# A cross-attention kernel on one core: the max rounds run four visits ahead of the exponent tiles instead of three

## The reference

```python
q, k, v = heads(x @ w_q), heads(text @ w_k), heads(text @ w_v)      # text: 1593 tokens
out_text = softmax(q @ k.T / sqrt(16)) @ v
out_ip   = softmax(q @ k_ip.T / sqrt(16) + mask) @ v_ip             # 8 tokens
out = (merge(out_text) + merge(out_ip)) @ w_out + b_out + x
```

## Time and profile before

| | |
|---|---|
| median of 3 runs (lowest to highest) | 1845.01 us (1843.49 to 1846.52) |
| profiled execution: its own time | 1848.91 us |
| profiled execution: span of the core's instructions | 1847.0 us |
| busy: PE, DVE, ACT, POOL | 1811.4, 1332.3, 1185.7, 382.6 us |
| mean granted TensorE clock | 0.993 |
| loop groups 0 to 38 begin | 79.88 to 1765.71 us after the span's start |

### The profile page before, as it was taken

One profiled execution on the slowest core, in us unless ns is written; L12 is line 12 of the kernel. 1 busy time (PEld: TensorE's weight loads), 2 busy tenths in 40 slices (PEclk: granted clock), 3 DMA queues, 4 the chain that ended last, 5 costly groups with the idle time before them and its releaser, 6 DMA issues.

```text
span 1847.0 us, 41069 instructions
## 1 busy us (share of the span) xinstructions
PE 1811.4 (98%) x16856; PEld 718.8 (39%) x16856; DVE 1332.3 (72%) x1787; ACT 1185.7 (64%) x2340; POOL 382.6 (21%) x508
## 2 busy tenths in 40 slices
PE   8999999999999999999999999999999999999988
PEld 3333333433344343433344333343333433434332
DVE  6777777778767787677876777777777777767871
ACT  1276666666666666666666666666666666666766
POOL 5112222211122121122121221112122122221000
PEclk9999999999999999999999999999999999999989
DMA  7555334363344434355453464435544364343410
GB/s 226 102 92 160 67 77 92 73 164 73 74 106 116 106 71 86 94 139 102 79 99 75 141 103 77 97 69 144 94 77 96 72 155 85 74 95 74 77 30 26
DMA packets 103806, 178.16 MB, mean 96 GB/s; under 512 B 42933, under 2 KB 71270, under 8 KB 103618
## 3 DMA queue, kind: packets, MB, share of 16 engines
q1 hardware_dynamic: 82658, 134.12, 37.3%
q0 software_dynamic: 18944, 40.10, 6.9%
q10 hardware_dynamic: 2016, 1.31, 0.2%
HBM read 117.63 MB, written 48.98 MB: 90 GB/s over the span
## 4 chain that ended last, share of the span: by engine, by line
PE 93%; DMA 2%; DVE 2%; SPq 1%; ACT 1%; issue 1%; POOL 0%; ACTq 0%; DVEq 0%; POOLq 0%
PE pv_bank L800 27%; PE max_bank L727 20%; PE work_bank L582 12%; PE exp_bank L784 12%; PE work_bank L604 11%; PE work_bank L627 3%; PE work_bank L593 2%; PE max_bank L745 2%; PE exp_bank L788 1%; DVE tile_max L1069 1%; DMA o_t<-o_sum 1%; SPq L475 1%; ACT probs L978 1%; PE work_bank L658 1%; PE work_bank L611 1%
## 5 line engine op out<-in xcount | busy, mean ns | idle before, releaser
L978 ACT ACTIVATE probs<-exp_bank 128x512 f32<-128x512 f32 x1908 | 1002.0, 599 | 417.3 <-PE exp_bank L784 410.2
L1069 DVE TENSOR_REDUCE tile_max<-max_bank 128x2 f32<-128x1024 f32 x632 | 773.4, 1224 | 400.5 <-PE max_bank L727 395.5
L727 PE MATMUL max_bank<-k_stack,q_stack 48*128 48x512 f32 x1896 | 567.9, 469 | 7.4 <-DVE tile_max L1069 7.3
L800 PE MATMUL pv_bank<-probs,v_ones 128*17 128x512 f32 x3840 | 518.1, 603 | 0.1
L1071 DVE TENSOR_REDUCE tile_max<-max_bank 128x1 f32<-128x512 f32 x632 | 430.2, 681 | 2.7 <-PE max_bank L727 2.7
L784 PE MATMUL exp_bank<-q_stack,k_stack 50*128 50x512 f32 x1908 | 415.9, 403 | 4.0 <-DMA q_stack<-neg_rows 2.7
L727 PEld LDWEIGHTS max_bank<-k_stack,q_stack 48*128 48x128 f32 x1896 | 234.0, 185 | 409.8 <-issue 269.6
L784 PEld LDWEIGHTS exp_bank<-q_stack,k_stack 50*128 50x128 f32 x1908 | 240.0, 188 | 63.2 <-ACT probs L978 47.2
L582 PE MATMUL work_bank<-ctxt,wk 128*32 128x400 f32 x2528 | 253.5, 506 | 7.6 <-DMA wk<-in_w_k 5.5
L604 PE MATMUL work_bank<-wv,ctxt 128*32 128x320 f32 x3040 | 254.0, 435 | 0.0
L604 PEld LDWEIGHTS work_bank<-wv,ctxt 128*32 128x32 f32 x3040 | 93.8, 109 | 163.1 <-issue 100.3
(11 more groups left out here) (124 smaller groups left out, 832.3 us busy)
## 6 DMA issues: line engine op xcount, KB each, us to landing
k_stack<-scratch_k SPq DMA_DIRECT2D x234, 199.2 KB, 6.9
scratch_k<-k_parts SPq DMA_DIRECT2D x80, 400.0 KB, 4.6
ctxt<-in_ctx_t POOLq DMA_DIRECT2D x28, 800.0 KB, 11.1
q_stack<-scratch_q SPq DMA_DIRECT2D x240, 64.0 KB, 2.3
scratch_q<-q_parts SPq DMA_DIRECT2D x80, 128.0 KB, 5.7
r_wide<-scratch_r POOLq DMA_DIRECT2D x39, 256.0 KB, 5.1
xres<-in_x SPq DMA_DIRECT2D x8, 640.0 KB, 9.0
out<-xres SPq DMA_DIRECT2D x32, 160.0 KB, 1.9
```

The source lines that it names most:

```text
L727: nc.tensor.matmul(round_place(n, r)[:, k, :], exact(q_stack[stack, slot, c, t * 128:(t + 1) * 128]), exact(k_stack[stack, slot, c, chunk ...
L800: last = nc.tensor.matmul(pv_bank[h * 32:h * 32 + VW, :], v_ones[:, v_slot(b, kt), head * VW:(head + 1) * VW], p, start=(kt == 0), stop=(k ...
L978: nc.scalar.activation(dst, exp_place(group_no, at), ACT.Exp, scale=SCALE).then_inc(probs_ready, 1)
L1069: nc.vector.reduce_max(flat[:, at:at + 2], place[:, 0:2, :], AX.X).then_inc(max_taken, 1)
```

## The change

`LEAD` goes from 3 to 4, and the prologue does one max round more, the last one beside the second half of the piece K(2,1).

```diff
-LEAD = 3
+LEAD = 4
...
-PRO_PLAN += [(("NEG", 0), ALL, 0)] + [(("K", 2, c), half, 1 - c * n) for c in range(2) for n, half in enumerate(HALVES)]
+PRO_PLAN += [(("NEG", 0), ALL, 0)] + [(("K", 2, c), half, 1) for c in range(2) for n, half in enumerate(HALVES)]
 assert sum(n for _, _, n in PRO_PLAN) == ROUNDS + LEAD
```

## The result

The changed kernel takes 1969.7 us (median of 4 runs, 1963.69 to 1973.84), the kernel before 1844.25 us (4 runs). The medians are 125.5 us apart; the ratio on record is 1.0688 with a 95% interval of 1.0668 to 1.0707, which makes 126.8 us of 1844.25. The direction and the main mechanism came as forecast; the size did not: 1969.7 lies above the range's end of 1965. The profiled execution took 1963.69 us, its span is 1961.9 us.

What follows compares the result with a forecast made beforehand. TensorE's own stream was taken as the bound. Terms: 107.9 - 4.4 + 5.4 + 2.3 + 0.7 - 1.0 - 3.1 - 5.7 = +102.1 us, on the median 1845.0: 1947 us, range 1930 to 1965.

Steps and rivals of the forecast that it cites:

- What bounds the kernel: TensorE, busy 98% of the span: the length of its own stream counts, visit by visit, not its few waits.
- Lost pairs: Round and visit of equal parity lose a matmul pair: net 469 more long blocks x 0.23, +107.9 us.
- what covers them: Visits without projection work, 29 in groups 1, 37, 38: VectorE sets the pace, two thirds of long blocks hidden, -4.4 us.
- the stalls that shrink: The first output weights' matmul (L693) waits 3.1 us less; visits where VectorE is late lose 5.7 us less.
- VectorE's lateness: Visits behind one with PV and no work find VectorE late; long blocks give it time, -5.7 us.
- The rest round in visit 13: Without PV there, next max tiles wait for VectorE: 0.17 us in 15 groups, 1.39 in two, together +5.4 us.
- 5.4 + 2.3 - 1.0: Waits behind the rest round, its first matmul exposed on the same side, and group 38 losing visit 13's round.
- Maxima: Ready a visit sooner, still turned in visit 14, so nothing follows: free.
- no pair is lost in the changed kernel: Rival 1: visit 15 is long for another reason, perhaps VectorE's end of the rest round; 1850 us, chance 0.04.
- the faster case: Rival 2: side order costs nothing and moving the rest round from beside PV saves 13 us; 1832 us, chance 0.03.
- The third: Rival 3: the new 1.39 us waits begin more stretches at TensorE's lower clock; 1985 us and more, chance 0.03.

Runs made afterwards that it cites:

- the two runs with turned sides: Heads taken in the order 0, 2, 1, 3 instead of 2, 0, 3, 1: in the changed kernel 1874.53 us, in the kernel before 1950.07 us.
- the run with the early copy: The changed kernel, with ScalarE copying the turned maxima in visit 14 behind its first exponent instead of its third: 1944.94 us, ratio 1.0575.

## Why the prediction was right in kind and wrong in size

**What bounds the kernel: right.** TensorE's own stream decides, and the two runs with turned sides show that the order of sides in it is worth 91 and 110 us.

**Lost pairs, with what covers them and the stalls that shrink: right.** The visits 0 to 11 grew by 94.5 us in all, measured over 39 groups from the first exponent tile of one visit to that of the next. The terms of the sum for them give 12 x 39 x 0.23 = 107.6 less 4.4, 3.1 and 5.7: 94.4 us. That the two agree to a tenth is luck: 13.2 us of these visits before and 10.2 us after stand at the lower clock, and counted at full clock they grew by 96.0 us. Nor does the total prove each of the three small terms. The wait of L693 fell by 3.2 us where 3.1 were forecast. The term for hidden blocks was too high: the 26 visits without work among 0 to 11 in the groups 1, 37 and 38 grew by 2.9 of 26 x 0.23 = 6.0 us, so about half was hidden and not two thirds. The count of 29 also leaves out visits 6 to 10 of group 0, which have no work either and grew by 0.8 of 1.15 us. The share of VectorE's lateness was not measured apart.

**The rest round in visit 13: right in kind.** In group 20 the V work of visit 13 takes 1063.88 - 1062.44 = 1.44 us to the next max tiles, instead of 1.22, where 0.17 more were forecast:

```profile
1062.44 1.28 PE L604 MATMUL work_bank<-wv,ctxt 128*32 128x320 f32 x16
1063.88 0.51 PE L727 MATMUL max_bank<-k_stack,q_stack 48*128 48x512 f32 x2 [0.16 <-DVE s_ip L1060]
```

The two groups without work wait 1.36 us where 1.39 were forecast, and K work shows no wait (1015.01 - 1013.53 = 1.48 us). But in the run with the early copy, visits 12 to 16 together take 13.38 us in the mean, counted at full clock, against 13.33 before. That is 2 us in 39 groups, where the terms for that stretch (one long block won and one lost, 5.4 + 2.3 - 1.0) make 7.0: they were too high by 5 us. Which of them is not shown.

**Maxima: this step failed.** The prediction says of the maxima that they are ready a visit sooner and still turned in visit 14, "so nothing follows from it", and that "ScalarE has slack". I followed when the turning's input is ready and who waits for its output in the next group. I did not follow what stands ahead of its copy in ScalarE's queue, nor that the projection work of the same visit waits for the bank. The rest round had been the cover: it delayed the turning until ScalarE was through with the exponents. Moving it to visit 13 took the cover away from its neighbour. The missing term is 36 x 0.57 = 20.5 us by the timeline, 20.8 us by the run that removes it. With it the sum is 102.1 + 20.5 = 122.6, or 1968 us. Counted at full clock, the two profiles are 121.6 us apart: 96.0 in the visits 0 to 11 (forecast 94.4), 23.5 in the visits 12 to 16 (forecast 7.0, with nothing for the copy), and 2.1 in the prologue (forecast 0.7). So 1968 comes so near to 1969.7 in part because small errors cancel, which is luck.

**The measure.** The profile of after has 13.7 us at the lower clock, that of before 27.3 us; the lower level is 1.2 instead of 2.4 GHz. If half of such a stretch is lost, the two profiles, 114.8 us apart as they stand, would be some 121.6 apart at an equal clock (an estimate). The four runs after took 1963.69, 1967.62, 1971.78 and 1973.84 us, at mean granted clocks of 0.997, 0.993, 0.991 and 0.989. The profiled execution is the shortest of the four, 6 us under their median, so the profiles show less of the loss than the medians do. The range's end of 1965 was passed by forecast and missing term together, 1968.

**The rivals.** That no pair is lost in the changed kernel, and the faster case built on it, are refuted by both runs with turned sides. The third, waits that pull the clock down, is not what made the loss: the four runs after have mean granted clocks of 0.989 to 0.997, the profile before has 0.993. One stretch of 3.4 us at the lower clock does begin 0.4 us behind the new wait of 1.36 us in group 37; behind the same wait in group 1 there is none, nor behind any of the short ones. In the run with the early copy such a stretch begins 0.5 to 0.9 us behind each of the two long waits. They are too few to count.

## What to carry to other kernels

Where matmuls on different rows of the array run in pairs, the order in which they are issued is a resource. Check a shift by one place for which partner each matmul then stands beside, and not only for waits; with an odd number of tiles to a round, here three, every shift by one round changes the pairing. When a block of work moves away, ask of each neighbour that stays what the block had been hiding, on every engine: here it hid ScalarE's exponents ahead of a small copy that frees the bank for the next work. And the loss by a wait is to be read from one fixed point to the next, not from the idle time shown.

## What the runs showed of the hardware that was not expected

TensorE's idle time ahead of the work in visit 14 is shown as 0.37 us, its start is 0.74 us later, and the visit is 0.57 us longer: three readings of one wait, of which only the last is the price. Where nothing waits, the V work overlaps with the end of PV, and takes 1.39 us to the next visit, against 1.22 us when it starts alone.

Two exponent tiles on one side ahead of the 66-column matmuls of the rest round cost nothing that the medians show (4.088 against 4.086 us), while a lost pair of 512-column matmuls costs 0.22 to 0.24 us.
